# A causal triangle added by VectorE in its maxima instead of by TensorE in two products

## The reference, cut to what matters

```python
scores = jnp.einsum('bhqd,bhkd->bhqk', q, k) / math.sqrt(dk)
causal = jnp.tril(jnp.ones((T, T), dtype=bool))
scores = jnp.where(causal, scores, -jnp.inf)
attn = jax.nn.softmax(scores, axis=-1)
out = jnp.einsum('bhqk,bhkd->bhqd', attn, v)
```

## Time and profile before

| | us |
|---|---|
| median of 3 runs | 1858.41 |
| lowest, highest run | 1853.79, 1865.11 |
| span of the profiled execution | 1867.2 |
| PE busy in it | 1647.8 (88%) |
| DVE busy in it | 1131.8 (61%) |
| ACT busy in it | 867.8 (46%) |
| POOL busy in it | 470.7 (25%) |

### The profile page before, as it was taken

One profiled execution on the slowest core, in us unless ns is written; L12 is line 12 of the kernel. 1 busy time (PEld: TensorE's weight loads), 2 busy tenths in 40 slices (PEclk: granted clock), 3 DMA queues, 4 the chain that ended last, 5 costly groups with the idle time before them and its releaser, 6 DMA issues. The chain is left out here.

```text
span 1867.2 us, 29072 instructions
## 1 busy us (share of the span) xinstructions
PE 1647.8 (88%) x10776; PEld 966.2 (52%) x10782; DVE 1131.8 (61%) x2567; ACT 867.8 (46%) x1358; POOL 470.7 (25%) x593
## 2 busy tenths in 40 slices
PE   4899999899999999954799999779998999998776
PEld 2344444478855666533456656456774344443533
DVE  2687777343245665647667776355454787774476
ACT  1266556533215555532135555447671566665322
POOL 4222120023313322010332230036772522200100
PEclk9799899999999999965899999979999999999699
DMA  7350441100064345000534532211114345320322
GB/s 243 88 142 35 108 119 23 68 1 0 1 175 128 85 120 159 2 9 0 155 93 129 142 114 47 77 52 52 52 52 139 99 105 158 88 71 1 122 91 91
DMA packets 68961, 160.30 MB, mean 86 GB/s; under 512 B 10285, under 2 KB 15926, under 8 KB 67962
## 3 DMA queue, kind: packets, MB, share of 16 engines
q1 hardware_dynamic: 68826, 158.51, 30.0%
HBM read 109.05 MB, written 53.09 MB: 87 GB/s over the span
## 5 line engine op out<-in xcount | busy, mean ns | idle before, releaser
L1078 DVE TENSOR_REDUCE a_mx<-PS 128x1 f32<-128x512 f32 (+3 forms) x768 | 395.0, 553 | 192.6 <-PE PS L1320 128.8
L1261 ACT ACTIVATE a_pT<-PS 128x1024 f32<-128x1024 f32 (+3 forms) x384 | 310.4, 812 | 214.8 <-PE PS L1344 151.7
L1315 PE MATMUL PS<-a_k,a_q 64*128 64x512 f32 (+3 forms) x768 | 231.9, 414 | 10.2 <-DVE a_mx L1078 6.1
L405 DVE CUSTOM_DVE_ANT_0 PS<-PS,a_dist 128x448 f32<-128x448 f32 x256 | 156.4, 644 | 62.9 <-PE PS L650 60.6
L1335 PE MATMUL PS<-a_q,a_k 64*128 64x512 f32 (+3 forms) x768 | 172.5, 435 | 6.8 <-issue 5.0
L1358 PE MATMUL PS<-a_pT,a_va 128*32 128x512 f32 (+3 forms) x1536 | 164.3, 499 | 5.6 <-ACT a_raw L1219 5.4
L555 ACT ACTIVATE a_pT<-PS 128x448 f32<-128x448 f32 (+1 forms) x256 | 124.6, 540 | 92.1 <-PE PS L673 91.8
L122 PE MATMUL PS<-cst 128*128 128x512 f32 x248 | 132.0, 661 | 37.7 <-PEq L66 28.7
L1315 PEld LDWEIGHTS PS<-a_k,a_q 64*128 64x128 f32 x768 | 110.1, 185 | 79.4 <-DVE a_mx L1078 60.7
L1335 PEld LDWEIGHTS PS<-a_q,a_k 64*128 64x128 f32 x768 | 74.9, 184 | 144.1 <-issue 68.5
L2074 POOL TENSOR_TENSOR f_h_low<-f_prod,f_h_high 128x512 fp32r<-128x512 f32 x84 | 111.5, 1334 | 60.8 <-ACT f_h_high L2261 55.6
(11 more groups left out here) (355 smaller groups left out, 3406.4 us busy)
## 6 DMA issues: line engine op xcount, KB each, us to landing
spread_scratch<-a_high SPq DMA_DIRECT2D x96, 256.0 KB, 3.4
a_q<-spread_scratch SPq DMA_DIRECT2D x96, 256.0 KB, 5.5
a_k<-spread_scratch SPq DMA_DIRECT2D x96, 256.0 KB, 6.2
f_gb<-gate_rows SPq DMA_DIRECT2D x68, 256.0 KB, 5.1
spread_scratch<-a_low SPq DMA_DIRECT2D x48, 256.0 KB, 4.1
a_q<-window_scratch SPq DMA_DIRECT2D x32, 256.0 KB, 5.4
a_k<-window_scratch SPq DMA_DIRECT2D x32, 256.0 KB, 6.0
window_scratch<-a_high SPq DMA_DIRECT2D x24, 256.0 KB, 4.7
```

The lines of the kernel that those rows point to most:

```text
L405: dve.tensor_tensor_reduce(PS[:, 4 + a, 0:KW], PS[:, 4 + a, 0:KW], dt_[:, off:off + KW], 1.0, 3e38, ALU.add, ALU.min, mx[:, gg % 2, qt, 2 ...
L1078: dve.tensor_reduce(mx[:, gg % 2, qt, 2 * half + a:2 * half + a + 1], PS[:, 4 + a, 0:kw], AX.X, ALU.max).then_inc(max_done, 1)
L1261: act.activation(pT[:, N // 2 % 2, N % 2, :, q0:S], PS[:, 2 * (N % 2):2 * (N % 2) + 2, q0:S], ACT.Exp, scale=SCALE).then_inc(exp_done, 1)
L1315: mm = pe.matmul(ps[:, 0:kw], q[rows, b % 2, pair, qt * P:(qt + 1) * P], k[rows, b % 2, pair, 0:kw], start=True, stop=not causal)
```

## The change

The score tiles of a1 and a2 lose their two mask products. GpSimd builds a table `tri` of 512 columns once per stage (384 zeros, then the triangle), and VectorE's reduction becomes the fused form of a0: it adds the last `kw` columns of `tri` to the tile, writes the sum back into the PSUM bank, and takes the maxima. VectorE waits once for the table, at its first tile. a3 keeps its plain reduction, and the transposed tiles keep their mask products. No instruction changes its place in the order.

```diff
+        tri = sb("tri", [P, S]) if causal else None
...
                 layer_norm_pool(pool, ln, 0, neg_half)
+                if causal:
+                    pool.memset(tri[:, 0:S - P], 0.0).then_inc(tri_done, 1)
+                    pool.tensor_tensor(tri[:, S - P:S], cst[:, C_MQ:C_MQ + P], zeros[:, 0:P], ALU.add).then_inc(tri_done, 1)
                 pool.wait_ge(ln.xn_done, TB)
...
+                    if causal and t == 0:
+                        dve.wait_ge(tri_done, 2)
                     dve.wait_ge(s_done, t + 1)
-                    dve.tensor_reduce(mx[:, gg % 2, qt, 2 * half + a:2 * half + a + 1], PS[:, 4 + a, 0:kw], AX.X,
-                                      ALU.max).then_inc(max_done, 1)
+                    out = mx[:, gg % 2, qt, 2 * half + a:2 * half + a + 1]
+                    if causal:
+                        dve.tensor_tensor_reduce(PS[:, 4 + a, 0:kw], PS[:, 4 + a, 0:kw], tri[:, S - kw:S], 1.0, -3e38,
+                                                 ALU.add, ALU.max, out).then_inc(max_done, 1)
+                    else:
+                        dve.tensor_reduce(out, PS[:, 4 + a, 0:kw], AX.X, ALU.max).then_inc(max_done, 1)
...
-                    ps = PS[:, 4 + a, :]
-                    mm = pe.matmul(ps[:, 0:kw], q[rows, b % 2, pair, qt * P:(qt + 1) * P], k[rows, b % 2, pair, 0:kw],
-                                   start=True, stop=not causal)
-                    if causal:
-                        pe.matmul(ps[:, kw - P:kw], half_masks[rows, 0, 0, :], half_masks[rows, 1, 0, :],
-                                  start=False, stop=False)
-                        mm = pe.matmul(ps[:, kw - 64:kw], half_masks[rows, 0, 1, :], half_masks[rows, 1, 1, 64:P],
-                                       start=False, stop=True)
-                    mm.then_inc(s_done, 1)
+                    pe.matmul(PS[:, 4 + a, 0:kw], q[rows, b % 2, pair, qt * P:(qt + 1) * P], k[rows, b % 2, pair, 0:kw],
+                              start=True, stop=True).then_inc(s_done, 1)
```

More of the change, by code:

```diff
@@ L830, in attention_quads @@
         preset, masks_done, y_started = sem("preset"), sem("masks_done"), sem("y_started")
+        tri_done = sem("tri_done")
         w_high_done, w_low_done = sem("w_high_done"), sem("w_low_done")
```

## The result

The changed kernel takes **1877.91 us** (median of 4 runs, 1874.17 to 1883.02), the kernel before beside it 1861.76 (4 runs): a ratio of 1.0095 [1.0063, 1.0127], slower by 0.6 to 1.3% (the ratio on record is worked out from the runs; the two medians alone give 1.0087). The forecast was 1844.5.

What follows compares the result with a forecast made beforehand. TensorE was taken to bound the causal stages, VectorE close behind. Gains of 6.7 us in a1, 4.3 in a2 and 2.8 in tiles ahead made 13.8, so 1858.4 became 1844.5 us; 8-in-10 range 1831 to 1873.

Steps and rivals of the forecast that it cites:

- 0.18 us go per pair that starts together: Causal 512-wide score pairs: without mask products TensorE's next work follows after 0.33 us instead of 0.51.
- VectorE's start: After a free 512 pair in a1 and a2: VectorE was to start 0.43 to 0.49 us after it, before 0.68.
- the half round's 0.24 us: Steps 4 to 7 of an a2 round: 0.24 us won, the next round starting at 1054.76 instead of 1055.00.
- the clock, left at 1.00 in the sum: TensorE's granted clock in a1 and a2 was expected to stay at 1.00, that is 2.4 GHz.
- The first rival: VectorE takes the path over: fused instruction and read do not overlap, 1.8 us a pair, 1881 us; chance 0.13.
- 0.42: Plain round of a1: 0.18 us from step 1 plus 0.24 from steps 4 to 7; 6.7 us over 16 rounds.
- The first round of a batch in a2: Where VectorE also rotates the next batch's projections: counted as +0.1 us a round.
- The tiles ahead: The 24 tiles ahead of each stage: about 10 pairs at 0.14 us, in two stages 2.8 us won.
- -13.8: Whole kernel: the summed gain of 13.8 us, from a1's rounds, a2's rounds and the tiles ahead.
- rival 3: Little comes of it: with a0's prices 0.08 us per free pair, about 0.2 a plain round, 1852 us; chance 0.26.
- Rival 2: TensorE's clock falls once per batch with a next one, both stages: 31 us lost, 1875 us; chance 0.10.

Runs made afterwards that it cites:

- e3: The kernel before without the two mask products, keeping its plain reduction, so maxima include masked keys: 1840.12 us, ratio 0.9916.
- e13: The changed kernel again, unmodified, beside the two versions with a filler product: ratio 1.0079 of the kernel before.
- e15: The changed kernel with one 512-column throw-away product ahead of each round's fifth step, where TensorE waits for nothing: ratio 1.0121 of the kernel before.
- e12: e3 with one 512-column throw-away product ahead of each causal round: ratio 0.9935 of the kernel before.
- e7: e3 with a one-column write by VectorE ahead of each causal maximum: ratio 1.0009 of the kernel before.
- e2: The changed kernel with TensorE's two mask products kept as well as the fused form: ratio 1.0094 of the kernel before.
- e11: The kernel before with one 512-column throw-away product ahead of each causal round: ratio 0.9987 of the kernel before.
- e4: The changed kernel with 512-column throw-away products: two ahead of each round, one between the score tiles of steps 0, 5 and 6: ratio 1.0108.
- e9: The changed kernel with one 512-column throw-away product in TensorE's wait ahead of each causal round: ratio 1.001 of the kernel before.
- e14: e9 repeated, beside the changed kernel: ratio 1.0027 of the kernel before.
- e10: e3 repeated without edits: ratio 0.9923 of the kernel before.
- e8: The changed kernel with the second, smaller mask product (64 columns wide) kept on TensorE: ratio 1.0084 of the kernel before.

## Why the prediction was wrong

Two steps of the prediction failed: "0.18 us go per pair that starts together", with VectorE's start after it, on which the half round's 0.24 us stood; and the clock, left at 1.00 in the sum. The first took away what was to be won, the second made the loss.

**The fused instruction was priced right.** A pair of 512 goes from 1048.34 to 1049.75, 1.41 us as forecast; the read and the next fused instruction start together at 1048.96, as in the earlier trace rows. The first rival's reading of the Trainium skill (VectorE: DVE Perf Modes, section "The DRAIN you can't avoid") left out that by the same section a next instruction that is not held starts earlier; the traces here agree with that half of it. That rival's 1.8 us did not come, but its place did: the rival was to decide from about 0.1 us over 1.41, and at 1.41 the fused form already costs 0.50 us a round (the changed kernel's 111.23 against e3's 107.75, over seven).

**What TensorE gives back was mis-sized.** The step "0.18 us go per pair that starts together" took a3's 0.33 us from the pair to the next work. It is 0.40 (1047.73 to 1048.13), which is nearer to a0's 0.40 at 448 columns, kept by the prediction for the range only: 0.11 are won, not 0.18. With it VectorE starts 0.61 us after the pair (1048.34), not 0.49. The likely reason, which no run tested by itself: the causal pair stands behind bf16 products of the transposed tile, as a0's stands behind bf16 products, and a3's does not. In the changed kernel's profile all 21 such pairs of a1 and a2 with values or a transposition behind them take 0.40 to 0.41 us, and a3's 19 with values behind them 0.32 to 0.33.

**So the half round wins 0.02 us, not 0.24.** From the start of step 4, forecast and measured: VectorE's first pair 0.78 and 0.91; values 2.67 and 2.80; the pair of 384 4.06 and 4.28; `keep_maxima` 5.20 and 5.45; the next round 6.56 and 6.78. The 0.13 at the first start has become 0.22 at the end; almost no gap on VectorE is left to take it up. Rounds of a1 win 0.10 us where 0.42 was forecast. Seven rounds of a2 at full clock, the third to the ninth, took 110.23 us before,

```profile
977.74:1087.97 110.23, 107.63 (x1080) 66.71 (x1081) 80.62 (x186) 58.09 (x87) 30.67 (x44) 1.00 0.46 120
```

and take 110.71 after:

```profile
976.68:1087.39 110.71, 102.44 (x856) 58.37 (x857) 86.75 (x298) 58.33 (x87) 30.66 (x44) 1.00 0.47 120
```

The first round of a batch in a2 grew from 14.69 to 14.96, forecast +0.1. The tiles ahead win 0.5 us a stage (a1: from 545.3 to 566.85 before, 539.0 to 560.08 now), forecast 1.4. At full clock the sum is about -1 to -2 us where it said -13.8: rival 3 holds for this part, and more than holds, so that without the clock the change would have come out level.

**The clock was put at 1.00, and that is the rest.** The steps of a1 and a2 take 487.3, 476.1, 480.6 and 487.1 us in four profiles of the changed kernel (mean 482.8) and 471.8 in both of before: 11 us. The end of a2 falls too, in all four: 10.83 us at a clock of 1.00 before,

```profile
1184.87:1195.70 10.83, 6.41 (x52) 4.37 (x50) 2.06 (x4) 2.21 (x5) 0.00 (x0) 1.00 0.00 0
```

and 13.78 at 0.75 after:

```profile
1186.02:1199.80 13.78, 9.36 (x52) 6.39 (x50) 2.06 (x4) 2.21 (x5) 0.00 (x0) 0.75 0.00 0
```

With the tiles ahead, 1 us shorter, the profiles place 13 of the 15 to 18 us measured (ratios of 1.008 and 1.0095).

The clocks on record show that the clock is all of the loss. The 86 runs of the kernel before have a mean clock of 0.949 and take 1859.5 us in the mean; the 17 of the changed kernel, from four measurements, have 0.936 and take 1873.1: 14 us more, with 48 us more at 1.2 GHz. At the same clock nothing is lost: between 0.940 and 0.942 lie four runs of before, 1869.2 us in the mean, and five of the changed kernel, 1867.7 (the former lose their clock outside these steps, as far as the two profiles of before show). The kernel before alone shows the price as well: its 22 runs at 0.952 to 0.955 take 1854.2 us, 15 less than those four, for 46 us less at 1.2 GHz. A microsecond at half clock costs a third of a microsecond.

Rival 2 named this and gave 1875, with a chance of 0.10. That this lies near 1877.91 is partly luck: it was 31 us lost, at a half for each at half clock, less the 14 to be won, where the runs show some 16 and 1 to 2. Its point against, that a3 waits eight times as long and keeps 0.99, carried too much weight. Its place was wrong as well: not one stretch of ten us per batch, but a few a stage; the 16 in the four profiles all begin 0.1 to 5.0 us behind the first product of a round.

That in the changed kernel filling the wait at a round's end gives back most of the loss, and the same work elsewhere none, is shown by e13 to e15. But this wait alone does not make the loss. In the steps of both stages TensorE's products wait at the start of rounds for 8.0 us in the changed kernel and for 8.0 in e3, which loses little clock; filling it there (e12, mean clock 0.945) changed nothing. What the changed kernel has besides is longer waits for maxima inside its rounds, 9.9 us against 2.6 in e3 and 1.0 before; but e7 has 2.9 and loses the clock too, so no single wait accounts for it. Both waits in a2 of the changed kernel:

```profile
PE PS L1325 <- DVE a_mx L1087: 6.4, 33, 0.7
PE PS L1339 <- issue: 4.2, 14, 0.3
```

Neither side of the change loses much clock by itself (e2 and e3); the two together do. What starts a stretch and what ends it is open. The mean clock falls with TensorE's unfilled time per round (length less busy, by modelled ends, over the seven rounds of a1), though not in every step:

| version | unfilled, us a round | mean clock | runs |
|---|---|---|---|
| e11 | 0.04 | 0.951 | 10 |
| before | 0.23 | 0.949 | 86 |
| e12 | 0.35 | 0.945 | 10 |
| e2 | 0.39 | 0.949 | 6 |
| e4 | 0.42 | 0.949 | 6 |
| e9, e14 | 0.51 | 0.945 | 22 |
| e3, e10 | 0.61 | 0.946 | 16 |
| e8 | 0.62 | 0.942 | 10 |
| e7 | 0.68 | 0.938 | 10 |
| e15 | 0.81 | 0.938 | 6 |
| changed | 0.83 | 0.936 | 17 |

**What the profile was to show.** Right: fused pairs of 1.41 us with overlapped reads, and waits for maxima above 3.8 us. Wrong: a1's and a2's windows (longer, not shorter), 0.33 behind a free pair, VectorE's start, waits under 20 us (24.6), and the clock (0.91 in a1).

## What to carry to other kernels

When work moves from the bounding engine to the one just behind it, run each side alone before trusting the sum, and look at the granted clock of both together: here the products were worth 0.60 us a round and the fused form cost 0.51, which adds up, but most of the clock was lost only where the two came together. The version that drops the products and adds nothing (e3, 0.9916) was the one worth having, because the softmax does not need the triangle in its shift, as long as no masked score lies far above the row's own. Price an instruction from the place whose neighbours ahead are of the same kind, not from the same line elsewhere. And where TensorE runs near its limit, short waits can cost more in granted clock than in waiting: here some 16 us against rounds that were no longer. A throw-away product that just fits into one of them is the test, and part of the cure; how the time of single runs goes with their clock says how much there is to win.

## What the hardware showed unexpectedly

- The Trainium skill (TensorE: Matmul & The Clock Gate, section "HAM oscillation — how this bites in real kernels") tells of pauses in TensorE's work that throttle the clock. Its example waits for DMAs between bursts of products; the runs agree in so far as a filled wait gave clock back (0.936 in e13, 0.945 in e14). What was not expected is how short the waits were: TensorE was busy 105.39 of 111.23 us in the rounds, with 0.30 us of wait at a round's end, and lost the clock three to six times in a profile; with that wait filled, once, though for 34 us.
- VectorE's write of one column ran beside the reduction behind it: both start at 1034.80, and the pair takes 1.30 us in place of 1.29.
- A stretch of 13.7 us at half clock cost its round 5.1 us, not the 6.8 that half of it would be, and over the runs such a microsecond cost a third of one. The slower TensorE has no waits left in the stretch (busy 13.59 of 13.70), which may be why; no run tests it.
